# A four-stage transformer kernel: its first batch prepared in two halves at once, the rotation by permuted partitions, and inverse roots in smaller pieces

## The chip, the cores and the metric

The kernel runs on one core of one Trainium2 chip. The metric is device time in microseconds (us), from the first to the last instruction of an execution with what lies around it. Three runs of the kernel before are known, and one more execution was profiled.

## What is computed

The input `x` has 4 batches of 1024 tokens with 128 channels. Six residual blocks follow each other; LN is the layer norm without scale.

```python
x = x + 0.5 * time_mix(LN(x))        # sigmoid(xr @ Wr.T) * (relu(xk @ Wk.T)**2 @ Wv.T); xr, xk mix each token with the one before
x = x + attention(LN(x)) @ proj      # 16 heads of 8, rotary positions, full softmax over 1024 keys
x = x + 0.5 * time_mix(LN(x))
x = x + 0.5 * experts(LN(x))         # rms norm, top 2 of 8 experts, u * silu(gate), plus skip
x = x + linear_attention(LN(x))      # softplus features, running sums
x = x + 0.5 * experts(LN(x))

def apply_rotary(x, cos, sin):
    x1 = x[..., ::2]
    x2 = x[..., 1::2]
    x_rot = jnp.stack((-x2, x1), axis=-1).reshape(x.shape)
    return x * cos + x_rot * sin
```

## The kernel before, in words

**Layout.** `x` stays in SBUF as 32 tiles of 128 tokens. Four tiles are a group of 512 tokens (`g`), two groups a batch. PSUM has 8 banks. Each engine runs its own program in order; a plan made when the kernel is built says which pieces of work come in which order, and every engine walks the same plan and does its share of each piece. Semaphores join the engines. Since each engine is in order, a piece that waits holds everything that stands behind it on its engine.

**The beginning** (`plan_start`, L283 to L298; `pe_start` L987, `dve_start` L1238, `act_start` L1269, `pool_start` L1357, `sp_attention` L1400). First groups 0 and 1 go through the first time mix: statistics, `factors` (VectorE writes variances at L580, GpSimd takes the power -0.5 of them at L593), `mn` (VectorE normalises, L604), `mt` (TensorE turns, L615, ScalarE copies, L747), `mk` (product L686/L687, VectorE clamps at L727, ScalarE squares at L751), `mr` (L692/L693, tanh at L755), `mv` (L698, VectorE L733, GpSimd adds to `x`, L767) and `ms` (statistics). ScalarE then fills four quarters of the score operands with ones (`act_blanks`, L1323 to L1331).

Then the queries and keys of batch 0 are prepared (`attention_queries`, L122). A piece is numbered `i` = 0 to 3: queries of half 0 and 1, keys of half 0 and 1. For each `i` there are two products (`rot`, L779), one for the values and one with swapped weight columns for the rotated neighbour; VectorE adds a bias and multiplies by the cosine or sine (L1131), GpSimd adds the two (`roped`, L1345). Then `split`: the float32 result becomes three bfloat16 parts in rounds. In batch 0 ScalarE rounds (L1289) and VectorE subtracts (L1149); in the other batches VectorE does both (L1154 to L1157). VectorE also squares (L1138), sums the keys (L1140) and takes the longest norm (L1161) from a product (`norms`). In batch 0 the pieces `i` follow one another through one pair of buffers `t_cos`, `t_sin`: a new piece waits until GpSimd has added the one before (L1129). SyncE writes the parts to DRAM (`write_parts`, L1410 to L1413: one transfer for each half-stack of queries, two for keys) and reads them back in the stacked layout of the score products (`stack_parts`, L1421): for batch 0 first two of the eight head pairs of queries and keys, 12 transfers, then the other six pairs, 12 transfers.

`bound` (L1209) works out a bound of the scores, `max` (L962, L1176) a shift for each row; ScalarE sends it to DRAM (L1387) and reads it into the stacked layout (`maxima_in`, L1397; in batch 0 at the piece `max_in`). Behind it stand, in this order, `mn` for groups 2 and 3, the values of batch 0 (`val`), and `mt`, `mk`, `mr`, `mv` for groups 2 and 3.

**Attention** (L997, L1250, L1293, L1364) has 256 steps. A step has two score units on TensorE (L1018, four matmuls), two exponentials of 1024 columns on ScalarE (L1307) and one sum over keys (L1035). Step 8 is the first that needs head pairs 2 to 7. `plan_attention` (L301) puts side pieces into the steps: the queries, keys and values of the next batch, the mixes of other groups, the second time mix, and the routing of the first round of experts. At most two pieces go into a step, and at most one of them may use TensorE. All side products share PSUM bank 7, so that a side product waits until VectorE or ScalarE has read the one before. A `rot` product is cut into two pieces that go into two steps.

**Routing** (`route_part`, L249). `rroot` lets GpSimd take the power -0.5 of two variances for each tile in one instruction (L586, L1675). `rnorm` waits for it, writes two rows of factors for the residual (`keep`, L1538, L1539), and normalises the tiles (L1545); then `rext` turns them on TensorE (L615) and `rscore` scores them (L1489). The linear attention asks for its factors through `lfac` in the same way.

## Time and profile before

| what | value |
|---|---|
| median of three runs | 1231.58 us (1227.18 to 1231.70) |
| the profiled execution, its own time | 1228.77 us |
| its span, from first to last instruction | 1227.0 us |
| mean granted TensorE clock | 0.932 of full speed |
| busy: TensorE, ScalarE, VectorE, GpSimd | 1023.1, 798.9, 602.1, 428.5 us |
| first exponential starts | 84.9 us |
| last exponential starts | 623.2 us |

Busy time counts neither waits nor the issuing of transfers. In the trace's rows PE is TensorE, PEld its weight loads, DVE VectorE, ACT ScalarE, POOL GpSimd, SP SyncE; "ACTq" is the sequencer of ScalarE issuing a transfer. "L1307" is a line of the kernel. A bracket at the end of a row of the timeline gives the time in which the engine stood idle before it, and what released it.

### The profile page before, as it was taken

How to read it: one execution, taken by the hardware profiler on the slowest of the kernel's cores; microseconds unless marked ns; L12 is line 12 of the kernel's file. 1: busy time of each engine (PE TensorE's matmuls, PEld its weight loads, DVE VectorE, ACT ScalarE, POOL GpSimd, SP SyncE). 2: the span in 40 equal slices, each digit the busy share in tenths (PEclk: the TensorE clock that was granted, in tenths of full speed). 3: DMA queues.
4: the chain of work that ended last, by engine and by line, in shares of the span. 5: the costliest groups of instructions: out<-in, count | busy, mean ns of one | idle time of the engine just before them, and what ended most of it. 6: DMA issues, size and time to landing. Idle time of an engine off the chain costs nothing.

```text
span 1227.0 us, 22947 instructions
## 1 busy us (share of the span) xinstructions
PE 1023.1 (83%) x8718; PEld 474.0 (39%) x8718; DVE 602.1 (49%) x1791; ACT 798.9 (65%) x1164; POOL 428.5 (35%) x406
## 2 busy tenths in 40 slices
PE   4479998998999989999978989888889875989930
PEld 3342222322222233222236656644445443665620
DVE  4753565366365234321234525757877943524522
ACT  4439888988899979999953646665455522565510
POOL 4211122221111211454211345544543483455445
PEclk9679999999999999999999989989999987998975
DMA  5180280027127600300101333200000011334422
GB/s 153 39 130 1 52 116 3 2 50 106 15 53 115 187 1 1 126 26 27 31 14 52 98 107 93 80 21 20 17 16 2 14 42 45 108 104 114 121 69 67
DMA packets 84826, 74.74 MB, mean 61 GB/s; under 512 B 11440, under 2 KB 78896, under 8 KB 83824
## 3 DMA queue, kind: packets, MB, share of 16 engines
q1 hardware_dynamic: 74924, 55.48, 19.9%
q0 software_dynamic: 8192, 16.79, 4.7%
q8 instruction: 74, 1.21, 0.4%
q10 hardware_dynamic: 1604, 0.99, 0.3%
q14 instruction: 32, 0.26, 0.1%
HBM read 39.28 MB, written 33.95 MB: 60 GB/s over the span
## 4 chain that ended last, share of the span: by engine, by line
PE 55%; DVE 18%; ACT 12%; POOL 5%; issue 4%; DMA 1%; ACTq 0%; POOLq 0%; SPq 0%; DVEq 0%
PE ps L1035 11%; PE ps L1755 11%; ACT attn_probs L1307 10%; PE ps L1018 6%; PE ps L779 6%; PE ps L1781 5%; PE ps L615 3%; PE ps L1767 2%; POOL moe_back L1700 2%; PE ps L2063 2%; DVE lin_scores L2191 2%; PE ps L1745 2%; PE ps L1987 2%; PE ps L2077 1%; DVE stats L571 1%
## 5 line engine op out<-in xcount | busy, mean ns | idle before, releaser
L1307 ACT ACTIVATE attn_probs<-ps 128x1024 f32<-128x1024 f32 x512 | 484.6, 1063 | 48.1 <-PE ps L1018 46.8
L1035 PE MATMUL ps<-attn_probs,attn_v 128*18 128x512 f32 x2048 | 271.9, 603 | 4.5 <-DVE room L1266 3.9
L1689 POOL DMA_INDIRECT slots<-moe_xr,moe_slot x128 | 125.9, 984 | 141.5 <-ACT attn_probs L1307 51.8
L1018 PE MATMUL ps<-stack 50*128 50x512 bf16 x1024 | 165.5, 387 | 7.4 <-ACT attn_probs L1307 1.3
L1700 POOL DMA_INDIRECT moe_back<-results,moe_slot x128 | 123.6, 965 | 103.8 <-PE ps L1745 43.4
L1755 PE MATMUL ps<-stack,lin_scores 128*128 x312 | 155.4, 621 | 0.0
L1018 PEld LDWEIGHTS ps<-stack 50*128 50x128 bf16 x1024 | 34.3, 94 | 242.9 <-ACT attn_probs L1307 229.1
L1861 ACT ACTIVATE lin_scores<-ps 128x256 f32<-128x256 f32 x156 | 58.4, 382 | 97.8 <-PE ps L1755 97.8
L1834 DVE TENSOR_TENSOR lin_scores<-ps,lin_scores 128x256 f32<-128x256 f32 x156 | 59.0, 419 | 113.7 <-ACT lin_scores L1861 113.6
L1781 PE MATMUL ps<-stack,lin_scores 128*128 x624 | 83.6, 276 | 4.8 <-ACT lin_heads_out L1874 4.8
L1781 PEld LDWEIGHTS ps<-stack,lin_scores 128*128 128x128 f32 x624 | 76.0, 192 | 6.5 <-issue 6.5
L1755 PEld LDWEIGHTS ps<-stack,lin_scores 128*128 128x128 f32 x312 | 56.0, 200 | 40.2 <-issue 40.1
L1035 PEld LDWEIGHTS ps<-attn_probs,attn_v 128*18 128x18 f32 x2048 | 45.7, 97 | 59.8 <-issue 39.0
L1345 POOL TENSOR_TENSOR room<-room 128x512 f32<-128x512 f32 x16 | 22.2, 1389 | 132.8 <-DVE room L1131 132.8
L2261 ACT ACTIVATE lin_scores<-ps 128x512 f32<-128x512 f32 x64 | 34.7, 595 | 42.1 <-PE ps L2063 42.1
L2191 DVE TENSOR_TENSOR lin_scores<-ps,c_causal 128x512 f32<-128x512 f32 x64 | 41.0, 682 | 35.2 <-PE ps L2063 35.2
L1827 DVE TENSOR_SCALAR lin_scores<-ps,c_norm_scale 128x256 f32<-128x256 f32 x80 | 37.9, 474 | 35.0 <-PE ps L1745 34.6
L1767 PEld LDWEIGHTS ps<-c_ident,lin_scores 128*128 128x128 f32 x312 | 38.5, 142 | 37.6 <-issue 35.0
L1131 DVE SCALAR_TENSOR_TENSOR room<-ps,c_attn_b,moe_xr 128x512 f32<-128x512 f32 x32 | 23.9, 749 | 58.9 <-PE ps L779 57.4
L1867 ACT ACTIVATE lin_scores<-ps 128x512 f32<-128x512 f32 x80 | 46.7, 584 | 7.6 <-PE ps L1767 4.8
L571 DVE BATCH_NORM_STATS2 stats<-x 128x6 f32<-128x128 f32 x192 | 41.4, 278 | 20.2 <-POOL x L897 8.8
L1745 PE MATMUL ps<-c_ident,moe_gathered 128*128 128x128 f32 x156 | 33.0, 294 | 20.0 <-DMA moe_gathered<-slots 13.1
(227 smaller groups left out, 1483.0 us busy)
## 6 DMA issues: line engine op xcount, KB each, us to landing
moe_gathered<-slots SPq DMA_DIRECT2D x76, 128.0 KB, 2.4
results<-lin_heads_out SPq DMA_DIRECT2D x76, 128.0 KB, 1.8
stack<-qk_parts SPq DMA_DIRECT2D x36, 256.0 KB, 9.4
qk_parts<-moe_xr SPq DMA_DIRECT2D x32, 128.0 KB, 2.5
qk_parts<-moe_xr SPq DMA_DIRECT2D x16, 192.0 KB, 2.8
stack<-in_expert_w SPq DMA_DIRECT2D x1, 3072.0 KB, 10.6
slots<-zeros SPq DMA_DIRECT2D x1, 3008.0 KB, 11.3
slots<-zeros SPq DMA_DIRECT2D x1, 2496.0 KB, 18.3
```

The costliest lines, as they stand in the source:

```text
L779: instruction = T.matmul(out[cols, :], weights[:, cols], moving, start=True, stop=True)
L1018: instruction = T.matmul(k.ps[:, SCORE_BANKS[i % 3][s], :], d.stack[b % 2][rows, 1, pair, kt * P:(kt + 1) * P], d.stack[b % 2][rows, 0, pa ...
L1035: instruction = T.matmul(k.ps[32 * j:32 * j + STRIP, PV_BANK, :], d.v[:, b % 2, kt, first:first + STRIP], d.probs[:, n % A_PROBS, j * BANK ...
L1307: A.activation(d.probs[:, n % A_PROBS, 2 * e * BANK:2 * (e + 1) * BANK], k.ps[:, banks[0]:banks[1] + 1, :].rearrange("p a n -> p (a n)"), ...
L1689: G.indirect_dma_start(out=k.dram["slots"][half][0:SLOT_TILES[r] * P], out_offset=bass.IndirectOffsetOnAxis(ap=d.slot[:, FIRST[r] + at, c: ...
L1700: G.indirect_dma_start(out=k.back[:, i % RING, c, :], out_offset=None, in_=k.dram["results"][half][0:SLOT_TILES[r] * P], in_offset=bass.In ...
L1755: T.matmul(k.ps[:, bank, :], d.gt[:, u % NB, i, :], w[:, bass.ds(offset[u, i], 2 * HIDDEN)], start=True, stop=True).then_inc(k.full[bank], 1)
L1767: instruction = T.transpose(k.ps[:, bank, at:at + P], d.h[:, u % NB, i, c * P:(c + 1) * P], k.ident[:, :])
L1781: instruction = T.matmul(k.ps[:, bank, i * DIM:(i + 1) * DIM], d.ht[:, u % NB, i, c * P:(c + 1) * P], w[:, 2 * HIDDEN + c * DIM:][:, bass. ...
L1834: V.tensor_tensor(d.h[:, u % NB, i, :], k.ps[:, bank, 0:HIDDEN], d.silu[:, u % NB, i, :], ALU.mult).then_inc(k.free[bank], 1)
L1861: A.activation(d.silu[:, u % NB, i, :], k.ps[:, bank, HIDDEN:2 * HIDDEN], ACT_FN.Silu).then_inc(k.e_silu, 1)
L2191: V.tensor_tensor(d.scores[:, m % NS, :].rearrange("p (j t) -> p j t", j=HPG), k.ps[:, bank, :].rearrange("p (j t) -> p j t", j=HPG), caus ...
```

## The change

All in one edit: (1) `plan_start` orders the beginning by hand. Both halves of a piece go side by side: two normalised buffers, and a second pair of rotation buffers for odd `i` (`rotated`). `split` is replaced in batch 0 by three pieces `cut` for each `i`, all squares and rounds on ScalarE, the subtractions on VectorE; the sum of the keys comes out of a round (`accum_out`). ScalarE copies the turned tiles and normalises groups 2 and 3 (from `shift`, a product made by VectorE), and clamps their `mk`. `mt`, `mk` and `mr` of groups 2 and 3 stand between the rounds, and only `mv` and the values follow `max`. (2) The fills by ScalarE are gone; SyncE writes just two rows of ones for each half of the two stacks, in four transfers. (3) The slots of queries and keys are exchanged, so that keys are written in one transfer for each half-stack. The stacked queries are read as soon as both halves have landed, and the other six pairs are read when the row shifts have landed. (4) In batches 1 to 3 the neighbour comes from `stream_shuffle` on VectorE, not from a second product. (5) Powers are taken in pieces: of at most 4 tiles for the first 8 of a request and then the rest, in routing the needed factor first in pieces of 8 tiles, the factor for `keep` last; the two `keep` rows move from `rnorm` to `rtop`.

```diff
+def first_queries():
+    def rotate(i, which):
+        return [("rot", 0, i, which, 0), ("rot", 0, i, which, 1)]
+    out = [("norm", 0, 0), ("norm", 0, 1), ("shift",), ("xt", 0, 0), ("xt", 0, 1), ("mn", 2), ("mn", 3)]
+    out += rotate(0, 0) + rotate(0, 1) + rotate(1, 0) + rotate(1, 1)
+    out += [("cut", 0, 0), ("cut", 1, 0)] + rotate(2, 0) + [("cut", 0, 1), ("cut", 1, 1)] + rotate(2, 1)
+    out += [("cut", 0, 2), ("cut", 1, 2), ("mt", 2), ("norms", 0, 0)] + rotate(3, 0) + [("mt", 3), ("norms", 0, 1)] + rotate(3, 1)
+    out += [("mk", 2), ("cut", 2, 0), ("mr", 2), ("cut", 2, 1), ("mk", 3), ("cut", 3, 0), ("cut", 2, 2), ("norms", 0, 2)]
+    return out + [("cut", 3, 1), ("norms", 0, 3), ("mr", 3), ("cut", 3, 2)]
...
-    k.start += [piece for _, piece in attention_queries(0)] + [piece for _, piece in attention_maxima(0)]
-    k.start += [("max_in",), ("mn", 2), ("mn", 3)] + [piece for _, piece in attention_values(0)]
-    k.start += [(kind, g) for kinds in (("mt",), ("mk", "mr"), ("mv",)) for g in (2, 3) for kind in kinds]
+    k.start += first_queries() + [("bound", 0), ("max", 0), ("mv", 2), ("mv", 3)] + [piece for _, piece in attention_values(0)]
...
     def rotate(i, which):
-        yield PRODUCT, ("rot", b, i, which, 0)
-        yield SAME_BANK, ("rot", b, i, which, 1)
+        if b and which:
+            yield OTHER, ("rot", b, i, which, 1)
+        else:
+            yield PRODUCT, ("rot", b, i, which, 0)
+            yield SAME_BANK, ("rot", b, i, which, 1)
...
+def root_parts(tiles):
+    cuts = sorted({min(at, tiles.stop) for at in (tiles.start, tiles.start + TPG, tiles.start + 2 * TPG, tiles.stop)})
+    return [slice(*pair) for pair in zip(cuts, cuts[1:])]
...
+            if b and which:
+                dve_need(V, k, k.neighbours_done)
+                V.scalar_tensor_tensor(d.t_sin[:, :], d.t_sin[:, :], bias[:, 2 * qk + 1:2 * qk + 2],
+                                       k.sin[:, half * BANK:(half + 1) * BANK], ALU.add, ALU.mult).then_inc(k.a_turned, 1)
+                return
...
+            if b:
+                k.neighbours_done = dve_mark(k, V.stream_shuffle(d.t_sin[:, :], k.ps[:, bank, :], NEIGHBOUR))
...
+            if part == 0:
+                A.wait_ge(k.a_roped, i + 1)
+                if i >= 2:
+                    bank, n = k.use["norms", 0, i - 2]
+                    A.wait_ge(k.full[bank], n + 1)
+                A.activation(d.square[:, s, :], d.roped[:, s, :], ACT_FN.Square).then_inc(k.a_square, 1)
...
+            if half and not b:
+                parts_landed(b, i)
+                stack_parts(b, qk, slice(0, 2), k.a_stack_first)
         if b == 0:
-            for qk in range(2):
-                parts_landed(b, 2 * qk + 1)
-                stack_parts(b, qk, slice(0, 2), k.a_stack_first)
+            S.wait_ge(k.a_max_in, 32)
             for qk in range(2):
                 stack_parts(b, qk, slice(2, PAIRS), k.a_stack_in[0])
...
-            pool_inverse_root(G, k, d.root[:, :, some], d.root_var[:, :, some])
+            pool_inverse_roots(G, k, [(d.root[:, 1, part], d.root_var[:, 1, part]) for part in parts]
+                               + [(d.root[:, 0, some], d.root_var[:, 0, some])])
```

## Rows read from the trace of the kernel before

**Rows 1.** The page: the costliest group of instructions.

```profile
L1307 ACT ACTIVATE attn_probs<-ps 128x1024 f32<-128x1024 f32 x512 | 484.6, 1063 | 48.1 <-PE ps L1018 46.8
```

**Rows 2.** By stretch: length, busy PE, PEld, DVE, ACT, POOL, granted clock, DMA share, GB/s.

```profile
0.00:84.40 84.40, 41.72 (x191) 31.19 (x192) 45.62 (x137) 30.27 (x29) 20.20 (x22) 0.80 0.48 109
...
139.50:435.00 295.50, 273.81 (x2901) 80.42 (x2901) 151.00 (x412) 263.78 (x282) 58.85 (x43) 0.99 0.39 71
```

**Rows 3.** Timeline of the beginning, until the first rounding: start, duration, instruction, idle before.

```profile
22.26 14.53 ACT L1331 ACTIVATE stack<-pair 32x4096 f32<-32x4096 f32 x4
...
27.40 2.91 POOL L593 TENSOR_TENSOR ln_rstd<-ln_var,minus_half 128x16 f32<-128x16 f32 x1 [1.61 <-DVE ln_var L580]
...
37.33 0.75 DVE L1131 SCALAR_TENSOR_TENSOR room<-ps,c_attn_b,moe_xr 128x512 f32<-128x512 f32 x1 [1.02 <-PE ps L779]
...
39.86 1.26 POOL L1345 TENSOR_TENSOR room<-room 128x512 f32<-128x512 f32 x1 [9.55 <-DVE room L1131]
41.16 0.63 ACT L1289 ACTIVATE moe_xr<-room 128x512 bf16<-128x512 f32 x1 [4.37 <-POOL room L1345]
```

**Rows 4.** The same timeline: last rounding, row shifts, values, last mix, first scores.

```profile
61.45 0.63 ACT L1289 ACTIVATE moe_xr<-room 128x512 bf16<-128x512 f32 x1 [0.76 <-DVE room L1149]
...
66.37 0.48 PE L962 MATMUL ps<-c_ident,attn_neg_max 128*128 128x128 f32 x1 [2.17 <-issue]
...
66.64 3.62 PE L779 MATMUL ps<-c_attn_vo,room 128*128 128x128 f32 x16
...
70.08 1.84 ACTq L1397 DMA_DIRECT2D stack<-row_maxima  x2
...
84.42 1.14 PE L1018 MATMUL ps<-stack 50*128 50x512 bf16 x6 [1.25 <-issue]
```

**Rows 5.** Stretches of 2 us, columns as in rows 2.

```profile
50.00:52.00 2.00, 0.20 (x1) 0.00 (x0) 1.30 (x3) 0.72 (x2) 0.00 (x0) 0.67 0.04 10
...
88.00:90.00 2.00, 2.00 (x10) 0.16 (x8) 1.95 (x13) 2.00 (x3) 0.00 (x0) 0.50 0.53 68
```

**Rows 6.** DMA issues from 40 to 110 us: size of one, median us to landing.

```profile
stack<-qk_parts SPq DMA_DIRECT2D x12, 192.0 KB, 10.5
...
stack<-qk_parts SPq DMA_DIRECT2D x12, 64.0 KB, 2.4
```

**Rows 7.** GpSimd's powers by shape, over the span: count, busy us, mean ns, idle before.

```profile
L593 POOL TENSOR_TENSOR ln_rstd<-ln_var,minus_half 128x8 f32<-128x8 f32 x9 | 14.9, 1655 | 25.6 <-DVE ln_var L580 25.6
...
L593 POOL TENSOR_TENSOR ln_rstd<-ln_var,minus_half 128x4 f32<-128x4 f32 x10 | 10.6, 1057 | 21.2 <-DVE ln_var L580 21.2
```

**Rows 8.** The chain that ended last, in order of time: start, length, what.

```profile
426.51 5.44 POOL moe_root L593
...
660.13 2.92 POOL moe_root L593
...
896.12 1.69 POOL ln_rstd L593
...
1024.43 2.94 POOL moe_root L593
```

**Rows 9.** Timeline of ScalarE: steps 108 to 133, and the first routing.

```profile
324.15 17.66 ACT L1307 ACTIVATE attn_probs<-ps 128x1024 f32<-128x1024 f32 x18 [0.52 <-PE ps L1018]
341.99 31.80 ACT L1307 ACTIVATE attn_probs<-ps 128x1024 f32<-128x1024 f32 x34 [0.17 <-PE ps L1018]
...
434.46 0.60 ACT L1648 ACTIVATE moe_xrt<-ps 128x512 f32<-128x512 f32 x1 [3.08 <-PE ps L615]
```

**Rows 10.** VectorE by line and shape, 140 to 435 us: count, busy us, mean ns.

```profile
L1155 DVE TENSOR_TENSOR room<-room,moe_xr 128x512 f32<-128x512 f32 x22 | 15.9, 725 | 0.8
...
L1157 DVE CAST moe_xr<-room 128x512 bf16<-128x512 f32 x11 | 4.7, 427 | 0.4
...
L1120 DVE COPY room<-ps 128x512 f32<-128x512 f32 x4 | 2.8, 690 | 2.9 <-PE ps L615 2.9
```

**Rows 11.** Timeline of TensorE: one side piece of a rotation product.

```profile
98.96 0.64 PE L779 MATMUL ps<-room,c_qk_w 128*32 128x256 f32 x8
```

More of the change, by code:

```diff
@@ L66 @@
 STACK = 64
+NEIGHBOUR = [(lane // HD ^ 1) * HD + lane % HD for lane in range(32)]
 PAIRS = HEADS // 2
@@ L721, in dve_mix @@
         instruction.then_inc(k.mix_weights, 1)
-    elif kind == "mn":
+    elif kind == "shift":
+        some = slice(DVE_MIXES * TPG, FIRST_MIXES * TPG)
+        V.wait_ge(k.root_out, max(k.root_of[t] for t in range(some.start, some.stop)))
+        V.scalar_tensor_tensor(d.shift[:, :], k.moments[:, some, 0], -1.0, k.rstd[:, some], ALU.mult,
+                               ALU.mult).then_inc(k.mix_shift, 1)
+    elif kind == "mn" and g < DVE_MIXES:
         dve_normalise(V, k, g, d.xn[:, g % 2, :, :], k.mix_xn)
-    elif kind == "mk":
+    elif kind == "mk" and g < DVE_MIXES:
         bank, n = k.use[kind, 0, g]
@@ L742, in act_mix @@
     kind, g = piece[0], piece[1] if len(piece) > 1 else None
-    if kind == "mt":
+    if kind == "mn" and g >= DVE_MIXES:
+        A.wait_ge(k.mix_shift, 1)
+        for i in range(TPG):
+            t = g * TPG + i
+            instruction = A.activation(d.xn[:, g % 2, i, :], k.x[:, t, :], ACT_FN.Identity, scale=k.rstd[:, t:t + 1],
+                                       bias=d.shift[:, t - DVE_MIXES * TPG:t - DVE_MIXES * TPG + 1])
+        instruction.then_inc(k.mix_xn_act, 1)
+    elif kind == "mt":
         b, at = g // 2, (g % 2) * BANK
@@ L911, in side @@
             T.wait_ge(k.a_xn, HALVES * b + piece[2] + 1)
-            pe_turn_group(T, k, piece, lambda i: d.xn[:, i, :])
-        elif kind == "rot":
+            pe_turn_group(T, k, piece, lambda i: d.xn_first[piece[2]][:, i, :] if b == 0 else d.xn[:, i, :])
+        elif kind == "rot" and piece[:4] in k.use:
             _, _, i, which, part = piece
@@ L1115, in side @@
         if kind == "norm":
-            dve_normalise(V, k, HALVES * b + piece[2], d.xn[:, :, :], k.a_xn)
-        elif kind == "xt":
+            dve_normalise(V, k, HALVES * b + piece[2], d.xn_first[piece[2]] if b == 0 else d.xn, k.a_xn)
+        elif kind == "xt" and b:
             half = piece[2]
@@ L1157, in side @@
             V.tensor_copy(d.parts[:, s, place[2], :], d.roped[:, s, :]).then_inc(k.a_parts, 1)
+        elif kind == "cut" and piece[2] < 2:
+            i, part = piece[1:]
+            s, place = i % 2, K_PLACE if i // HALVES else Q_PLACE
+            V.wait_ge(k.a_rounded[s], 2 * (i // 2) + part + 1)
+            V.tensor_tensor(d.roped[:, s, :], d.roped[:, s, :], d.parts[:, s, place[part], :],
+                            ALU.subtract).then_inc(k.a_less[s], 1)
         elif kind == "norms":
```

162 lines of the change are left out of this document (88 added, 74 removed).

## Prediction

> **What bounds the kernel now.** I read the page first, then the busy time by stretch, the timeline up to the first exponential, the chain, and the waits of ScalarE. The costliest group is the exponentials [rows 1]: 512 of them, 484.6 us, all between 84.9 and 624 us, so for 540 of the 1227 us ScalarE's exponentials set the pace, with 48.1 us of idle time between them, nearly all put down to the score products. Two things follow: each us by which the first exponential comes earlier is a us of the kernel, and TensorE's side work counts only where it makes ScalarE wait. Before the first exponential no engine is full [rows 2]: in 84.4 us VectorE is busy 45.6, TensorE 41.7, ScalarE 30.3. That is a chain of short steps. A last kind of place is GpSimd's powers: six of those of 8 columns or more stand in the chain (four are shown, [rows 8]; the others are at 92.4, 1.65 us, and 988.1, 2.95), while everything behind them waits.
>
> **The beginning, part by part.** The first power (8 tiles) is cut into 4 and 4: 1.66 becomes 1.06 [rows 7], so all that follows is 0.6 earlier. The second, of 16 tiles, took 2.91 [rows 3]; now the first 4 tiles are ready after 1.06. It starts at 26.8, ends at 27.9, and VectorE normalises both halves back to back (1.1 us each, to 30.1) since they have two buffers. TensorE turns them by 31.2; ScalarE copies (0.6). At the slow clock a rotation product takes 1.7 us (35.4 to VectorE's start at 37.33 [rows 3], two hops in it), so VectorE has both products of piece 0 at 35.0 and GpSimd adds by 37.1, against 41.1 before: 4.0 earlier. The fills, 14.5 us of ScalarE [rows 3], go; I cost that at nothing, since they ended at 36.8 and ScalarE then sat idle 4.4 us for GpSimd's sum. What they covered is now filled by eight small normalisations, some 3 us, which end at 34.9. Their replacement, four transfers by SyncE, stands behind SyncE's loads (over by 17 us) and before its first parts at 43: 25 us for four transfers, nothing on the path.
>
> From 37.1 ScalarE has 24 instructions up to the last round: four squares, twelve rounds, two copies and two clamps for groups 2 and 3, two squares and two tanh. At 0.64 us (a round takes 0.63 [rows 3]) that is 15.4 us, or 52.5 if it never waited. It will wait: for VectorE's subtraction between rounds (0.73 [rows 10], partly covered by the other half), for GpSimd's sums of pieces 2 and 3, and, being in order, for the `mk` and `mr` products that stand between the rounds. Walking the four queues with these durations I get 58.0 with TensorE at full clock throughout, and 62.4 with it at half clock through `mk` and `mr` of group 2 and `mk` of group 3 (each then 3.4 instead of 1.7 us). The clock fell at 50 to 52 us after TensorE had little to do [rows 5], and the same gap now comes at 41 to 44, before dense work, so I take a point between, 59.5. Before, it was 62.1 [rows 4]: 2.6 us gained, with 8.6 us of mixes already inside.
>
> The way from there to the row shifts is unchanged, 4.3 us (62.1 to 66.4 [rows 4]); the maximum's turn is then at 63.8. Behind it stood 18.0 us: values 3.6, the landing of the shifts, and groups 2 and 3 from `mt` to `mv`, the scores at 84.42 [rows 4]. Now only `mv` twice and the values stand there. At half clock: 0.5 for the turn, 3.7, 3.6, then VectorE 0.9 and 0.5 to start the scores, 9.2 in all. The shifts land at about the same time: 1.1 to VectorE's end, 2.6 for the transfer out, 1.8 to issue two transfers [rows 4], 2.3 to land, 7.8. So scores at 73.0 instead of 84.4: **11.4 us gained**, with ends 8.5 (half clock, 75.9) and 14.3 (full clock, 7.8 behind the maximum, 70.1).
>
> The other six head pairs now wait for the shifts. Before, 12 transfers of 192 KB were issued from 70.7 and the engines were still 53% busy at 88 to 90 us [rows 5], 18 us later; the median landing was 10.5 us, against 2.4 for the small ones [rows 6]. Now the first issue is at about 71.6, the last landing at 89 to 90. Step 8 needs it; before, it came 16.5 us after the first scores, here 89.5. I charge **1 us**, with ends 0 and 3. The keys' own first pairs are no danger: written (1.2), landed (2.5), read (2.9 to issue, 2.4 to land) they are there 9 us after the last round, at 68.5.
>
> **Rotation.** In batches 1 to 3, 24 side pieces of TensorE go, 0.64 us of work each [rows 11]. What one costs ScalarE: in steps 108 to 116, with such a piece in nearly each, two exponentials took 1.96 us, in 117 to 133 1.87 [rows 9], so at least 0.1, 2.4 us in all; at most its own 0.64, 15 us. I take 0.25 each, 6 us: nearer the low row, since other pieces move up into the free steps. VectorE gets 12 shuffles, for which the trace has no row. A copy of the same size out of PSUM takes 0.69 [rows 10]; a lower bound is a cast of this size within SBUF, 0.43 [rows 10], an upper one GpSimd's pass over two operands, 1.26 [rows 3]. I take the copy, the one with the same source, size and engine. At 0.69 VectorE gets 8.3 us more on 151 in 295 [rows 2]: half hidden by idle time, but the side bank is now held for 1.4 instead of 0.75 us, and behind a `split` (six passes) that makes a product late. I charge 1. **Net 5**, ends -3 and 12. The Trainium skill, "VectorE: DVE Perf Modes" (the perf-mode tier table), gives a shuffle one element a cycle, 2400 ns for 2048; by that estimate 0.6 us for 512, and the sum would not move.
>
> **Smaller powers.** At 426.5 us 32 columns took 5.44 [rows 8]; the first part will have 8, 1.66 [rows 7], and the two `keep` instructions (0.25) leave the path: 4.0. ScalarE, which had exponentials in hand, stood idle 3.1 us there [rows 9], and the chain runs through the power, so I count 3.1 at least and take 4.0. At 660, 988 and 1024 us 16 columns become 8: 1.3 each, with `keep` 1.5, 1.7 and 1.5. At 92 and 896 us 8 become 4: 0.6 each. Sum 9.9, all on the chain. GpSimd's total grows (three powers for one), but the rest runs while VectorE normalises. What may be late next is the DMA behind routing, so I take **8.5**, ends 5 and 10.
>
> **The sum.** 11.4 - 1 + 5 + 8.5 = 23.9 us, from the profiled execution's 1228.8 us to **1205 us**. That execution is 2.8 below the median of the three runs, which reach from 1227.2 to 1231.7, so a comparison with the median may look 3 us kinder. A difference over 0.5%, 6 us, can be told here.
>
> **Rivals.**
> A, the half clock. The mixes now come in a gap-filled stretch, TensorE stays at 1.2 GHz, in-order ScalarE waits at `mk` and `mr` and the rounds end at 62.4. For it: the clock fell at 50 to 52 us [rows 5], and its mean up to 84.4 us was 0.80 [rows 2]. Gains 8.5 in the beginning, rotation 2, powers 6, less 1, so 15.5: 1213. The Trainium skill, "TensorE: Matmul & The Clock Gate" (what's actually happening), says that the slow clock is the default and that activity releases it. Chance 0.2.
> B, the late stacks. Twelve large transfers behind the shifts take longer than 18 us or their issue slips; TensorE stands at step 8 for up to 8 us: 1212. Against it: the queue is emptier than before, since the small transfers are over. Chance 0.1.
> C, everything lands. Full clock, 14.3; side work was dearer than I think, 10; powers 10: 1195. Chance 0.15.
> D, slower: a shuffle out of PSUM costs far more than a copy. Its place is steps 6 to 130, its price the queue on VectorE behind bank 7. All else gains 25 (11.4 - 1 + 6 + 8.5), so the kernel is slower from 2.1 us a shuffle if each is fully exposed; at 3 us it would be 36 us against 25, 1240. Against it: the 512-column rows of VectorE stand at 0.43 to 0.73 [rows 10]. Chance 0.04.
> E, it does not do what it says: the freed steps are filled by the plan, the beginning hits a wait that I did not see, and 4 us are left: 1225. Chance 0.06.
>
> **How the numbers follow.** The forecast has 0.45, its own range is 1198 to 1211. With A, B and C the range is 1192 to 1218 and leaves out D, E and the tails of A and B, a little under 2 in 10. Faster by over 0.5%: all but D, half of E and the tails, 0.91; same 0.05; slower 0.04.
>
> **What would show it.** First exponential at 73 to 74 us, the last round at 58 to 60, first GpSimd sum of a rotation at 36. Twelve shuffles near 0.7 us. Idle time before L1307's group down from 48 to about 40 us, no row of 5.4 us among the powers and ScalarE's wait of 3.1 us at the first routing gone. A wait of the scores for a transfer at step 8 would mean B; half clock until 70 us and an idle ScalarE before the tanh of group 2, A. Attention as long as before with more time between products and VectorE would prove the rotation term wrong.

## Result and the profile after

The changed kernel takes **1201.92 us** (median of 4 runs, 1199.60 to 1203.07); the kernel before, on the same chip, 1230.90 (4 runs, 1227.18 to 1231.70). The ratio is 0.9768 with a 95% interval from 0.9753 to 0.9783: 2.3% faster. The profiled execution took 1201.29, its span 1199.5. Forecast were 1205, range 1192 to 1218.

A step is a pair of exponentials. Counted through the timeline of ScalarE, the steps start at (us):

| step | before | after | lead |
|---|---|---|---|
| 0 | 84.9 | 69.7 | 15.2 |
| 8 | 102.8 | 89.9 | 12.9 |
| 40 | 172.6 | 168.5 | 4.1 |
| 80 | 258.4 | 257.0 | 1.4 |
| 128 | 364.5 | 349.6 | 15.0 |
| 158 | 425.8 | 411.2 | 14.6 |
| 168 | 452.6 | 434.5 | 18.1 |
| 255 | 622.3 | 601.0 | 21.4 |
| from the last exponential's start to the end | 603.7 | 597.6 | 6.1 |

So the beginning gained more than forecast, most of it was gone by step 80, it came back by step 128, and routing and the rest added to it.

**The beginning**, timeline after, up to the last rounding, against [rows 3, 4]:

```profile
26.40 3.66 POOL L614 TENSOR_TENSOR ln_rstd<-ln_var,minus_half 128x4 f32<-128x4 f32 x3 [1.61 <-DVE ln_var L596]
...
31.32 3.17 ACT L774 ACTIVATE attn_probs<-x,mix_shift,ln_rstd 128x128 f32<-128x128 f32 x8
34.36 1.27 POOL L1398 TENSOR_TENSOR room<-room 128x512 f32<-128x512 f32 x1 [4.29 <-DVE room L1183]
35.66 0.63 ACT L1341 ACTIVATE room<-room 128x512 bf16<-128x512 f32 x1 [1.16 <-POOL room L1398]
...
55.86 0.62 ACT L1350 ACTIVATE moe_xr<-room 128x512 bf16<-128x512 f32 x1
```

The power of 16 tiles is now cut into 4, 4 and 8 (the row merges the three and names the first one's shape). The first GpSimd sum starts at 34.4 (before 39.9), the last round ends at 56.5 (before 62.1). From there to the scores, TensorE's timeline and ScalarE's queue:

```profile
60.51 0.48 PE L999 MATMUL ps<-c_ident,attn_neg_max 128*128 128x128 f32 x1 [2.20 <-issue]
...
69.23 0.82 PE L1056 MATMUL ps<-stack 50*128 50x512 bf16 x6 [1.30 <-DMA stack<-row_maxima]
...
89.47 0.60 PE L1056 MATMUL ps<-stack 50*128 50x512 bf16 x4 [3.51 <-DMA stack<-qk_parts]
```

The first scores wait last for the row shifts' landing, and start 8.7 us behind the turn of the maxima. The third line is step 8: TensorE stood 3.51 us for the second issue of stacks. The chain has both landings:

```profile
65.35 3.58 DMA stack<-row_maxima
...
73.92 15.51 DMA stack<-qk_parts
```

Twelve issues of 192 KB are 2.36 MB, let go at 68.95, when the shifts are in, and landed at 89.43. By stretch (columns as in [rows 2]; the last two lines are the 4 us behind the wait):

```profile
0.00:69.20 69.20, 40.88 (x190) 31.37 (x191) 36.05 (x120) 22.95 (x43) 21.04 (x24) 0.88 0.41 110
69.20:90.00 20.80, 14.83 (x108) 3.53 (x108) 11.64 (x55) 15.29 (x17) 5.27 (x5) 0.92 0.87 115
...
90.00:92.00 2.00, 2.00 (x26) 0.58 (x24) 0.00 (x0) 1.84 (x2) 0.00 (x0) 0.64 0.04 8
92.00:94.00 2.00, 2.00 (x24) 0.86 (x24) 0.00 (x0) 1.09 (x2) 0.00 (x0) 0.50 0.00 0
```

In the second line the DMA engines are 87% busy at 115 GB/s: 2.36 MB at that rate are 20.5 us, which is 68.95 to 89.4. In the third the granted clock is 0.64 and in the fourth 0.50: behind the wait TensorE ran for a time at the lower of its two levels, 1.2 GHz. ScalarE's timeline shows its own wait at step 8 and the one that follows it:

```profile
82.39 3.90 ACT L1368 ACTIVATE attn_probs<-ps 128x1024 f32<-128x1024 f32 x4 [0.86 <-PE ps L1056]
89.91 1.94 ACT L1368 ACTIVATE attn_probs<-ps 128x1024 f32<-128x1024 f32 x2 [3.61 <-PE ps L1056]
92.91 1.94 ACT L1368 ACTIVATE attn_probs<-ps 128x1024 f32<-128x1024 f32 x2 [1.06 <-PE ps L1056]
```

**The exponentials, the shuffles, the powers**, from the page and the groups by shape:

```profile
L1368 ACT ACTIVATE attn_probs<-ps 128x1024 f32<-128x1024 f32 x512 | 481.3, 1081 | 58.3 <-PE ps L1056 57.9
...
L1181 DVE STREAM_SHUFFLE room<-ps 128x512 f32<-128x512 f32 x12 | 8.9, 741 | 0.0
...
L614 POOL TENSOR_TENSOR ln_rstd<-ln_var,minus_half 128x4 f32<-128x4 f32 x30 | 30.7, 1033 | 61.5 <-DVE ln_var L596 61.5
...
L614 POOL TENSOR_TENSOR moe_root<-moe_root_var,minus_half 128x8 f32<-128x8 f32 x12 | 19.8, 1659 | 10.1 <-DVE moe_root_var L1587 10.0
```

The exponentials' idle time rose, 48.1 to 58.3, but 13.2 of it now is the wait ahead of the first one, 3.9 before; between exponentials it is about the same (45.1 and 44.2). The shuffle took 0.74 us; a power of 4 columns 1.03, of 8 columns 1.66. No power of 32 columns is left, and ScalarE no longer waits 3 us at the first routing.

### The profile page after: what moved, and what is told of

Its sections match the earlier page's. It is cut to its first block, busy times and chain, and to the rows that moved or that the text cites. A ratio compares the mean times of both kernels' runs of the same rounds, so it can differ in the third digit from the quotient of the medians.

```text
span 1199.5 us, 22563 instructions
## 1 busy us (share of the span) xinstructions
PE 1006.0 (84%) x8494; PEld 470.1 (39%) x8526; DVE 602.7 (50%) x1798; ACT 787.4 (66%) x1178; POOL 434.8 (36%) x425
## 4 chain that ended last, share of the span: by engine, by line
PE 52%; ACT 18%; DVE 17%; issue 4%; POOL 4%; DMA 3%; SPq 0%; POOLq 0%; ACTq 0%; DVEq 0%
ACT attn_probs L1368 16%; PE ps L1820 11%; PE ps L1073 9%; PE ps L1846 5%; PE ps L816 5%; PE ps L1056 5%; PE ps L636 3%; PE ps L1832 3%; POOL moe_back L1765 2%; PE ps L2128 2%; DVE lin_scores L2256 2%; PE ps L1810 2%; PE ps L2052 1%; PE ps L2142 1%; DMA stack<-qk_parts 1%
## 5 line engine op out<-in xcount | busy, mean ns | idle before, releaser
L1368 ACT ACTIVATE attn_probs<-ps 128x1024 f32<-128x1024 f32 x512 | 481.3, 1081 | 58.3 <-PE ps L1056 57.9
L1056 PE MATMUL ps<-stack 50*128 50x512 bf16 x1024 | 167.7, 387 | 13.2 <-DMA stack<-qk_parts 3.5
L1073 PEld LDWEIGHTS ps<-attn_probs,attn_v 128*18 128x18 f32 x2048 | 43.2, 97 | 64.8 <-issue 44.8
L614 POOL TENSOR_TENSOR ln_rstd<-ln_var,minus_half 128x4 f32<-128x4 f32 (+1 forms) x31 | 32.4, 1055 | 61.5 <-DVE ln_var L596 61.5
L1810 PE MATMUL ps<-c_ident,moe_gathered 128*128 128x128 f32 x156 | 33.1, 294 | 22.0 <-DMA moe_gathered<-slots 14.6
## 6 DMA issues: line engine op xcount, KB each, us to landing
slots<-zeros SPq DMA_DIRECT2D x1, 3008.0 KB, 12.9
```

The lines of the kernel that those rows point to most:

```text
L1056: instruction = T.matmul(k.ps[:, SCORE_BANKS[i % 3][s], :], d.stack[b % 2][rows, 1, pair, kt * P:(kt + 1) * P], d.stack[b % 2][rows, 0, pa ...
L1073: instruction = T.matmul(k.ps[32 * j:32 * j + STRIP, PV_BANK, :], d.v[:, b % 2, kt, first:first + STRIP], d.probs[:, n % A_PROBS, j * BANK ...
L1368: A.activation(d.probs[:, n % A_PROBS, 2 * e * BANK:2 * (e + 1) * BANK], k.ps[:, banks[0]:banks[1] + 1, :].rearrange("p a n -> p (a n)"), ...
```

## Experiments

The kernels ran in three groups, each on a chip of its own, so each kernel is compared through the kernel before, run beside it: 1242.52 us (17 runs) for e1 to e4, 1229.49 (13 runs) for e0, e5, e8, e9, and 1230.13 (7 runs) for e7, e10, e11, e12. Spans and step times are of one profiled execution each. "Behind it" is the time from the start of the last exponential to the end.

| kernel | median us | ratio [95%] | step 0 | step 158 | last exponential | behind it |
|---|---|---|---|---|---|---|
| after, again (e0) | 1204.25 | 0.9788 [0.9764, 0.9811] | 68.6 | 411.1 | 601.7 | 599.7 |
| e1 products | 1219.51 | 0.9798 [0.9764, 0.9832] | 71.1 | 415.7 | 609.6 | 608.1 |
| e2 routing powers | 1228.87 | 0.9869 [0.9834, 0.9905] | 69.6 | 417.8 | 611.0 | 618.2 |
| e3 no wait | 1222.52 | 0.9821 [0.9788, 0.9853] | 85.4 | 426.8 | 618.7 | 612.0 |
| e4 before, no fills | 1244.45 | 1.0015 [0.9995, 1.0035] | 84.4 | 424.7 | 626.0 | 616.6 |
| e5 mixes behind | 1209.34 | 0.9838 [0.9821, 0.9855] | 77.6 | 416.2 | 606.8 | 600.6 |
| e7 two shuffles | 1213.78 | 0.9856 [0.9826, 0.9885] | 70.8 | 420.7 | 611.4 | 602.5 |
| e8 second part first | **1193.84** | **0.9709** [0.9693, 0.9725] | 70.1 | 405.3 | 595.9 | 596.8 |
| e9 before, wait | 1229.73 | 1.0002 [0.9992, 1.0012] | 84.7 | 425.4 | 622.8 | 603.9 |
| e10 all powers | 1213.54 | 0.9861 [0.9831, 0.9892] | 72.9 | 417.6 | 608.3 | 604.0 |
| e11 ahead | 1199.44 | 0.9758 [0.9741, 0.9774] | 71.0 | 404.7 | 595.3 | 596.7 |
| e12 cut, products | 1200.44 | 0.9767 [0.9744, 0.9789] | 69.2 | 407.0 | 599.6 | 598.4 |

Two limits of this table. The profiled execution of e3, 1232.53 us, was the slowest of its five; the other four took 1218.61 to 1223.34. And the changed kernel has no run in the third group. e11, which differs from e8 only in the order of its transfers and has the same span within 0.7 us, has a ratio 0.0049 higher (6 us). So a comparison across groups, as of e7 and e10 with e0 or of e12 with e8, may be off by as much, and is held against the step times below.

**e0, the changed kernel again.** No edit.

> The changed kernel again, beside the kernels of this call, since chips differ by some us. Every theory: 0.977 of the kernel before, first exponential at 69.7 us of the trace, step 8 at 89.9 after a wait of 3.6 us.

Measured: 0.9788, step 0 at 68.6, a wait of 3.38 us at step 8 (88.5). The first exponential moves by 1.1 us from one execution to another.

### What makes the start early

**e4** is the kernel before with its fills done by four DMAs.

```diff
-        if piece == ("mr", 1):
-            act_blanks(A, k)
...
+            S.dma_start(stack[row:row + MAX_ROWS, 1, :, :].rearrange("p r (n c) -> p (r n) c", c=P), ones).then_inc(k.a_blank, 16)
```

> The kernel before with one thing changed: ScalarE's four fills replaced by SyncE's four transfers of ones. My theory: nothing, within 0.1% of the kernel before, since ScalarE only waits behind the fills. Rival: the fills slow VectorE or GpSimd by the memory they share, and the beginning is 1 to 3 us shorter without them.

Measured: no difference that the runs can tell, first exponential at 84.4. 14.5 us of ScalarE's work at the start were free, as the prediction had them.

**e3** takes the wait for the row shifts out of SyncE's queue, so that the second issue of stacks goes ahead of them. SyncE's own rows are written all the same; the scores wait for all they read.

```diff
-            S.wait_ge(k.a_max_in, 32)
```

> The changed kernel without SyncE's wait for the row shifts ahead of the stacks of pairs 2 to 7. In the changed kernel ScalarE stands idle 3.6, 1.1 and 0.6 us at steps 8 to 10, and the chain runs through that transfer. My theory: the twelve large transfers are issued from 62.7 us, land by 82, ahead of step 8, and the kernel is 4 to 5 us faster than the changed one, about 1197.5. Rival: they then stand in the way of the shifts (two small transfers), so that the first scores come later by what step 8 gains: 1201 to 1203.

Measured: the first exponential at 85.4, 15.7 later than in the changed kernel, although the turn of the maxima comes only 0.3 later. Its chain:

```profile
62.02 2.73 DMA row_maxima<-c_same_head
...
66.01 18.54 DMA stack<-row_maxima
84.55 0.14 issue
84.69 0.62 PE ps L1056 x2
```

The second of two transfers of 32 KB, issued at 66.01, took 18.5 us, against 3.6 with the wait. Seven of the twelve large stack transfers had been issued on SyncE's queue by then, the other five followed up to 68.8, and the shifts landed at 84.55, the last stack at 85.08. So it is not only the bytes ahead of them: the shifts were in almost last. Step 8 does not wait here, and in this execution the start lost stays lost: the last exponential is at 618.7, 16.9 later. But the ratios of all runs put e3 only 0.003 to 0.005 above the two measurements of the changed kernel, 4 to 7 us, with overlapping intervals, and this execution was 10 us above the median of its own five. Whether the shifts land as late in the other four is not known.

**e9** asks the opposite: is the wait alone enough? It is the kernel before with that one line added in front of its second issue of stacks.

```diff
+            S.wait_ge(k.a_max_in, 32)
             for qk in range(2):
                 stack_parts(b, qk, slice(2, PAIRS), k.a_stack_in[0])
```

> The kernel before with the one wait added: SyncE's queue issues the second part of the stacks only once the shifts have landed. Theory 'two locks': TensorE works through the mixes until 83.2 anyway, so the first exponential stays at 84 to 85 and the time within 0.4% of the kernel before; with e3 (mixes ahead, no wait: 85.4) this says that neither part alone brings anything. Rival 'the shifts' landing alone held the start': first exponential 2 us or more earlier, at the end of TensorE's mixes plus nothing (82 to 83), 2 us faster. Rival 'late stacks': the second part lands after step 8 (102.8) and the kernel is slower by 1 to 4 us; issued from about 76 and landing some 20 later (96), it should not.

Measured: 1.0002, first exponential at 84.7. TensorE still has its mixes up to 83, in front of the scores in its queue:

```profile
81.67 1.16 PE L698 MATMUL ps<-c_mix_w,attn_probs 128*128 128x128 f32 x8 [0.78 <-DVE attn_probs L733]
84.11 1.32 PE L1018 MATMUL ps<-stack 50*128 50x512 bf16 x6 [1.28 <-issue]
```

**e5** puts the mixes of groups 2 and 3 back behind the turn of the maxima in the changed kernel; the wait stays.

```diff
-    out += [("cut", 0, 2), ("cut", 1, 2), ("mt", 2), ("norms", 0, 0)] + rotate(3, 0) + [("mt", 3), ("norms", 0, 1)] + rotate(3, 1)
+    out += [("cut", 0, 2), ("cut", 1, 2), ("norms", 0, 0)] + rotate(3, 0) + [("norms", 0, 1)] + rotate(3, 1)
...
-    k.start += first_queries() + [("bound", 0), ("max", 0), ("mv", 2), ("mv", 3)] + [piece for _, piece in attention_values(0)]
+    k.start += first_queries() + [("bound", 0), ("max", 0)] + [piece for _, piece in attention_values(0)]
+    k.start += [(kind, g) for kinds in (("mt",), ("mk", "mr"), ("mv",)) for g in (2, 3) for kind in kinds]
...
```

> The changed kernel with the mixes of groups 2 and 3 (transposes, ranks, values) behind the turn of the maxima, where the kernel before had them; the wait of SyncE's queue for the shifts stays. Theory 'two locks': the start needs both, the mixes out of the way and the shifts ahead of the large transfers. Then the shifts land at about 65 but TensorE works through some 17 us of mixes (66.4 to 83.7 in the kernel before) from about 60.5 on: first exponential at 77 to 80, step 8 without a wait because the stacks landed meanwhile, and 5 to 8 us above the changed kernel. Rival 'the wait alone did it' : first exponential at 69 to 72 here too, time within 2 us of the changed kernel. Rival 'mixes only moved': ScalarE has the mixes' work to do either way and what is gained at the start is lost to idle time later, so the end differs by under 2 us although the start is 8 later.

The edit has one more part, not shown above: ScalarE reads the shifts in (`maxima_in`) right behind sending them out, ahead of the mixes, so that they land at 65.3. Measured: first exponential at 77.6, 9.0 later than e0. The stacks are in before step 8, so the wait of 3.4 us there is gone. Of the 9.0, 2.4 come back up to step 8 and 1.5 more up to step 80; the last exponential is 5.1 later, the time 5.1. With e3, e9 and this one the start is a lock with two keys. Mixes ahead, shifts ahead: 69.7. Mixes ahead alone: 85.4. Shifts ahead alone, in the old order: 84.7. In these executions each key alone moved the start by nothing. The other 7 us of the lead, 77.6 against 84.7, are what else the beginning has: both halves side by side, the smaller power, fewer waits between rounds; of these only the power was taken back by itself (e10 below, 3.1 to 4.3 us).

### The wait at step 8

**e8** cuts the second issue of stacks in two. Pairs 2 and 3 land on a semaphore of their own, which TensorE asks for at step 8; pairs 4 to 7 follow, asked for at step 16.

```diff
+            T.wait_ge(k.a_stack_second, STACK_IN)
+        if b == half == kt == 0 and group == 2:
             T.wait_ge(k.a_stack_in[0], STACK_IN)
...
             for qk in range(2):
-                stack_parts(b, qk, slice(2, PAIRS), k.a_stack_in[0])
+                stack_parts(b, qk, slice(2, 4), k.a_stack_second)
+            for qk in range(2):
+                stack_parts(b, qk, slice(4, PAIRS), k.a_stack_in[0])
...
```

> The changed kernel with the second issue of stacks cut in two: pairs 2 and 3 (12 transfers of 64 KB) right behind the shifts, pairs 4 to 7 (12 of 128 KB) behind them, and TensorE waits for the first part at step 8 and for the second at step 16. Theory 'the last landing holds step 8': the 3.6 us wait at step 8 goes, its 1.1 us follower at step 9 with it; step 8 at 86 to 87, step 16 about 4 earlier, and 1 to 4 us of it left at the end (side work crowds steps 19 to 40, so part of the lead may be given back there). Rival 'side work sets the pace to step 40': step 8 is 3.6 earlier but step 40 is not, and the time is within 1 us of the changed kernel. Rival 'the second part now lands after step 16': the wait only moves there; 12 large transfers issued by about 79 and landing 10 to 15 later would be in by 94, before step 16 at 103, so this one is unlikely.

Measured: 1193.84 us, **10.4 less than e0** beside it, far more than any theory had. Of the spans' 8.7, 5.8 stand up to the last exponential and 2.9 behind it. ScalarE's timeline:

```profile
82.99 5.87 ACT L1370 ACTIVATE attn_probs<-ps 128x1024 f32<-128x1024 f32 x6 [0.53 <-PE ps L1058]
89.06 11.78 ACT L1370 ACTIVATE attn_probs<-ps 128x1024 f32<-128x1024 f32 x12 [0.21 <-PE ps L1058]
101.25 7.44 ACT L1370 ACTIVATE attn_probs<-ps 128x1024 f32<-128x1024 f32 x8 [0.41 <-PE ps L1058]
```

Neither step 8 nor step 16 waits. Step 0 to step 8 takes 16.8 us instead of 19.9, step 8 to 40 74.3 instead of 78.6; from there on the two keep their distance. (e8's first exponential was 1.5 later than e0's, so its lead is 5.9 at step 40 and 5.8 at 158 and not 7.4.) So the uncut transfer cost 3.1 up to step 8, about the wait itself, and 4.3 more behind it: the waits at steps 9, 20 and 36, 1.0 to 1.2 each in e0, are gone with it, and the granted clock from 90 to 115 us is 1.00 against 0.91. How the 4.3 divide between the clock and those waits is not shown.

**e11** is e8 with pairs 2 and 3 issued ahead of the wait, and only pairs 4 to 7 behind it (the edit is against e8).

```diff
+            for qk in range(2):
+                stack_parts(b, qk, slice(2, 4), k.a_stack_second)
             S.wait_ge(k.a_max_in, 32)
-            for qk in range(2):
-                stack_parts(b, qk, slice(2, 4), k.a_stack_second)
```

> The kernel with the second issue of stacks cut in two (pairs 2 and 3, pairs 4 to 7), but pairs 2 and 3 (12 transfers of 64 KB) issued ahead of the wait for the shifts, only pairs 4 to 7 behind it. Theory 'bytes in the rings hold the shifts': without any wait 2.3 MB (12 of 192 KB) stood ahead of them and they landed 18.5 us after their issue; here 0.77 MB are issued by about 65 and are nearly through when the shifts are issued, so the shifts land 4 to 8 us after their issue, the first exponential is at 70 to 74, and the time is within 2 us of the kernel that has both behind the wait or up to 4 above it. Rival 'any transfer of stacks in flight holds them as long': first exponential at 80 to 85 and 8 or more above.

Measured: the shifts land 4.62 us after their issue, the first exponential is at 71.0. So 0.79 MB in twelve transfers around them held them by 1 us, 2.36 MB in twelve by 15; in both cases about half of the twelve had been issued before the second shift transfer (six here, seven in e3). The time is unclear: the profiled span is 1192.0, as in e8, but that was the fastest of five runs, the median is 1199.44 (1193.88 to 1201.18), and the ratio lies above that of e8 beyond both intervals, on another chip. I don't claim either order of the two.

### Rotation

**e1** is the changed kernel with the second product back in all batches; **e12** does the same to e8, where no wait at step 8 is in the way.

```diff
-        if b and which:
-            yield OTHER, ("rot", b, i, which, 1)
-        else:
-            yield PRODUCT, ("rot", b, i, which, 0)
-            yield SAME_BANK, ("rot", b, i, which, 1)
+        yield PRODUCT, ("rot", b, i, which, 0)
+        yield SAME_BANK, ("rot", b, i, which, 1)
...
-                k.neighbours_done = dve_mark(k, V.stream_shuffle(d.t_sin[:, :], k.ps[:, bank, :], NEIGHBOUR))
...
```

> The changed kernel with the rotation of batches 1 to 3 by a second product again, in the plan and on the engines. My theory: the 24 side pieces of TensorE cost ScalarE some 6 us and the shuffles gave 1 back, so this kernel is 5 us slower than the changed one, about 1207, with the first exponential still at 69.7 us. Rival: the rotation gave nothing, because the shorter plan crowds the side work and VectorE is late instead (ScalarE waits 2 to 3 us at steps 19, 31, 34 and 35 in the changed kernel): 1201 to 1203.

> The kernel with the second issue of stacks cut in two, and the rotation by a second product in all batches, as the kernel before had it. Without the wait at step 8 the rotation's worth is read by itself. Theory of the prediction's term: 3 to 7 us above the kernel with the stacks cut and the shuffles (ratio to the kernel before 0.974 to 0.977). Rival 'the shuffle's 0.74 eats it': the same within 2 us. Rival 'it was more': over 8 above, since 24 pieces of TensorE's side work also pushed others into stalls.

Measured: e1 lies 0.001 to 0.003 of the ratio above the two measurements of the changed kernel, inside the intervals. e12 against e8 is clearer: 6.6 us by the medians, 7.1 by the ratios (0.0058 of 1230), 5.3 by the spans, 3.7 up to the last exponential, 4.6 from step 0 to 255. The medians and ratios cross groups; against e11, on its own chip, e12's median is only 1.0 higher. The step times are the firmer figure. Four kernels side by side, each with one part more than the one to its left (us of the step times):

| from step to step | before | e12: + start, powers | e8: + shuffles | e0: + stacks uncut |
|---|---|---|---|---|
| up to 0 | 84.9 | 69.2 | 70.1 | 68.6 |
| 0 to 80 | 173.5 | 170.6 | 181.0 | 188.2 |
| 80 to 158 | 167.4 | 167.2 | 154.2 | 154.2 |
| 158 to 255 | 196.6 | 191.7 | 189.8 | 189.8 |
| from the start of step 255 to the end | 604.6 | 599.3 | 597.7 | 600.6 |

This is where the lead went by step 80 and where it came back. The shuffles make the first 80 steps 10.4 us slower and the next 78 13.0 faster: the plan has fewer products to place and sets the others earlier (the last rounding of batch 3's keys falls into step 124 instead of 131). So the total moves little and its place much. The uncut stacks cost another 7.3. e12 has the exponentials at the old rhythm:

```profile
L1360 ACT ACTIVATE attn_probs<-ps 128x1024 f32<-128x1024 f32 x512 | 484.6, 1064 | 52.9 <-PE ps L1055 51.5
```

Its 484.6 us are those of [rows 1], to the tenth.

**e7** does each shuffle twice, the second over the first.

```diff
+                dve_then(V, k, V.stream_shuffle(d.t_sin[:, :], k.ps[:, bank, :], NEIGHBOUR))
                 k.neighbours_done = dve_mark(k, V.stream_shuffle(d.t_sin[:, :], k.ps[:, bank, :], NEIGHBOUR))
```

> The changed kernel with each of its 12 shuffles done twice, one behind the other: 12 times 0.74 us of VectorE more, 8.9 in all, and the PSUM bank that the shuffle reads is held 0.74 longer. Theory 'VectorE has room in attention': under 3 us above the changed kernel (ratio to the kernel before up to 0.981), the extra time lying in idle time of VectorE. Rival 'VectorE's chain holds TensorE in the crowded steps 19 to 40': step 0 to step 158, 341.5 us in the changed kernel, becomes 346 to 350, and the time is 5 to 9 above.

```profile
L1181 DVE STREAM_SHUFFLE room<-ps 128x512 f32<-128x512 f32 x12 | 8.9, 740 | 0.0
...
L1182 DVE STREAM_SHUFFLE room<-ps 128x512 f32<-128x512 f32 x12 | 8.7, 729 | 0.0
```

Measured: 0.9856, which is 8.4 us above e0 by the ratio; step 0 to step 158 takes 349.9 us, against 342.5 in e0 and 341.5 in the changed kernel. By the step times, 7.4 to 8.4 of the 8.7 us of added shuffles came out, most of it (5.8 against e0) in the first 80 steps. The rival's size is right, though VectorE is busy only half of the time (161.0 of 295 us in the changed kernel from 115 to 410). Its mechanism, that VectorE's chain holds TensorE's bank and with it the scores, fits; the run lengthens both VectorE's work and the bank's hold, and does not tell them apart.

### Powers

**e2** joins routing's powers again (both halves in one instruction); **e10** also the norms'.

```diff
-            pool_inverse_roots(G, k, [(d.root[:, 1, part], d.root_var[:, 1, part]) for part in parts]
-                               + [(d.root[:, 0, some], d.root_var[:, 0, some])])
+            pool_inverse_roots(G, k, [(d.root[:, :, some], d.root_var[:, :, some])])
...
-    cuts = sorted({min(at, tiles.stop) for at in (tiles.start, tiles.start + TPG, tiles.start + 2 * TPG, tiles.stop)})
-    return [slice(*pair) for pair in zip(cuts, cuts[1:])]
+    return [tiles]
...
```

> The changed kernel with the powers of the routing in one instruction of both roots again (the keep factors stay where the change put them). My theory: 3.8 us at the first routing and 1.3 at each of three later ones come back, 7.7 in all: about 1209.5. Rival: what the powers gave was swallowed by the transfers behind the routing, and only the first counts: 1205 to 1206.

> The changed kernel with every power whole again, those of the norms (16, 12 and 8 columns in one instruction) and those of routing (both halves joined), as in the kernel before. Theory of the prediction's term: 5 to 10 us above the changed kernel. Rival from the earlier run with routing's powers alone joined, in which step 158 came 6.6 us later than in the changed kernel and step 255 9.3 later: 10 to 14 us above (ratio 0.985 to 0.989), 8 to 9 of it around the first routing (steps 152 to 168) and 2 to 5 behind attention. Rival 'norms alone are the term': step 255 as in the run with the joined routing powers (610.5 there), and only the part behind attention longer.

Measured: e10's ratio is 0.9861, 9.0 us above e0 (0.0073 of 1230) and 11.4 above the first measurement of the changed kernel (0.0093). Its beginning is 3.1 to 4.3 later (72.9; the power of 16 columns is back, 2.91 us); steps 0 to 152 are 2.4 shorter than in e0 (327.1 against 329.5). Then 4.7 is lost between steps 152 and 158 (17.7 us against 13.0), at this chain, which the changed kernel does not have:

```profile
404.91 0.09 DVE moe_root_var L1589
405.00 0.07 issue
405.07 5.44 POOL moe_root L616
410.51 0.03 issue
410.54 1.12 DVE moe_xr L1602 x4
```

From there to step 255 e10 and e0 take the same (189.8). Behind the last exponential it is 604.0 against 597.6 and 599.7. In the first group e2 lost more at the first routing, 6.9 from step 152 to 158 and 1.3 more up to 168. The clock is part of it: in e2 it stood at 0.50 in each stretch of 4 us from 408 to 420.

```profile
412.00:416.00 4.00, 4.00 (x20) 2.07 (x20) 0.19 (x1) 1.94 (x2) 0.00 (x0) 0.50 0.00 0
416.00:420.00 4.00, 4.00 (x23) 1.00 (x16) 0.00 (x0) 2.21 (x3) 0.00 (x0) 0.50 0.00 0
```

That is e2; and this is e10, whose clock was at 1.00 again by the second stretch:

```profile
412.00:416.00 4.00, 4.00 (x23) 1.46 (x21) 0.67 (x3) 1.45 (x2) 0.00 (x0) 0.64 0.00 0
416.00:420.00 4.00, 3.94 (x31) 1.13 (x30) 0.19 (x1) 3.43 (x6) 0.00 (x0) 1.00 0.00 0
```

Why e2's stayed down is not shown.

## Why the prediction was right, term by term

| term | predicted | measured | by |
|---|---|---|---|
| beginning | -11.4 (-8.5 to -14.3) | -15.2 | first exponential |
| step 8 | +1 (0 to 3) | +7.3 from step 0 to 255, +10.4 between medians | e8 against e0 |
| rotation | -5 (+3 to -12) | -4.6 from step 0 to 255, -6.6 between medians | e12 against e8 |
| powers, behind the beginning | -8.5 (-5 to -10) | -4.7 at routing, -4.3 to -6.4 behind attention | e10 |
| first 80 steps, same pieces | none | -2.9 | e12 against before |
| fills | 0 | 0 | e4 |
| sum | -23.9 | -29.0 (medians), -27.5 (spans) | |

**The beginning** was 3.8 better than forecast, 0.9 beyond the better end of its term. The working said: first sum ready at 37.1, last round ended at 59.5, scores at 73.0. It was 35.6, 56.5 and 69.2. The first 1.5 are VectorE's: GpSimd's sum could start at 34.4. The walk through the four queues at full clock allowed 20.9 us for the rounds (37.1 to 58.0), and 20.8 is what they took (35.66 to 56.48); the 1.5 added for the half clock was not due. The clock did fall at 42 to 46, as the forecast had it for 41 to 44, but it was up at 0.95 in the next 2 us and at 1.00 from 48 on, while the first dense products ran (`mk` of group 2, 45.1 to 47.5, took 2.4 us where 1.7 or 3.4 were reckoned with):

```profile
44.00:46.00 2.00, 2.00 (x6) 1.22 (x5) 0.98 (x2) 0.00 (x0) 0.00 (x0) 0.50 0.85 200
46.00:48.00 2.00, 2.00 (x10) 1.28 (x9) 0.13 (x1) 0.42 (x1) 1.26 (x1) 0.95 0.77 183
48.00:50.00 2.00, 2.00 (x14) 1.55 (x14) 0.00 (x0) 1.97 (x6) 0.00 (x0) 1.00 0.19 55
...
64.00:66.00 2.00, 2.00 (x12) 2.00 (x11) 0.41 (x1) 0.00 (x0) 0.77 (x1) 0.50 0.04 4
```

So **rival A** fell. The Trainium skill, "TensorE: Matmul & The Clock Gate" (what's actually happening), has the clock released by activity; the trace agrees, 0.50 at 44 to 46 us with TensorE busy throughout, then 0.95, and 1.00 from 48 to 58. The walk was worth more than the allowance on top of it. From 60 to 66 us, behind little work on TensorE (0.4 us in 56 to 60), the clock was at 0.50 again, as the forecast's last stretch had it. 4.0 and 8.7 to the turn and to the scores (4.3 and 9.2 forecast) gave the rest.

What the prediction did not see is why the start could move at all. It counted the landing of the shifts as 7.8 behind the maximum, "about the same time" as the rest, with 2.3 for the landing itself. No row gave it that: in the kernel before the second shift transfer took 7.5 us, to 78.8, 12.4 behind the turn, and only the mixes up to 83 hid it. The prediction did not say that without the wait in SyncE's queue the shifts could hold the scores until 84.6 (e3). It treated that wait only as a cost, the 1 us at step 8. That the number held without this reasoning is in part luck: the change had both keys.

**Step 8** is the term that failed. The landing was forecast at 89 to 90 and was 89.43, but by two errors that cancel: the transfers were issued at 68.95 and not at 71.6, and took 20.5 us and not 18. The 18 came from DMA engines still 53% busy at 88 to 90 us [rows 5]; in the same trace the first of the twelve is issued at 70.4 and the last lands at 92.4, 22 us. And the need was put 16.5 us behind scores at 73.0, so at 89.5, and scores came at 69.2; the need was at 86, the landing did not move with it, and 3.5 us of the better start were given back on the spot. About as much again was lost behind it: half clock at 90 us, then waits at steps 9, 20 and 36. The term was mis-sized in three ways: the transfers' time was read too short, the need depended on the start's own error, and a wait of TensorE was priced at its length. **Rival B** had its mechanism right (the twelve large transfers took longer than 18 us, and the scores waited at step 8). It allowed a wait of up to 8 us; the wait was 3.5 and its whole cost 7.3. It did not show as 1212 because the start and the powers gave more.

**Rotation**: the net was right and both of its parts were too low. The shuffle took 0.74 where the copy's 0.69 was taken. The estimate of 0.6 that the prediction worked out from the Trainium skill, "VectorE: DVE Perf Modes" (the perf-mode tier table), was under both. But the charge of 1 us for twelve, "half hidden by idle time", is refuted: 8.7 us more of them cost some 8 (e7). If the first shuffle of a pair costs what the second does, the 24 side pieces were worth some 12 to 15 us, near their upper end of 15 (0.64 each) and not 6. That last number is argued from e7 and e12, not measured alone; a second shuffle stands directly behind the first, and the first might have had more cover. The prediction's sign, idle time between exponentials down from 48 to about 40 us, did not come: without the wait ahead of the first it was 44.2 and is 45.1. **Rival D** asked for 2.1 us a shuffle and had 0.74. Its condition, that each is fully exposed, came nearly true for the added ones.

**Powers**: 9.0 to 11.1 where 8.5 were forecast and 9.9 was the sum of the rows. The first routing was to give 4.0; it gave 4.7 in steps 152 to 158 (e10). The four behind attention were to give 5.3 before the discount; with all powers whole that part is 4.3 to 6.4 longer. That part differs by as much between kernels with the same powers (see Open), so whether the discount for "the DMA behind routing" was needed is not settled.

**The sum** came out 3.1 under the forecast, inside its own range of 1198 to 1211. The start was 3.8 better and step 8 6.3 dearer than forecast. The terms as measured by steps add up to 24.4 to 26.5 of the 27.5 us between the spans; 2.9 of them are a term that the prediction lacked. **Rival C** had the start and the powers about right, but the wait at step 8 took back what it needed for 1195. e12 has the products' old pieces and yet runs the first 80 steps in 170.6 us instead of 173.5. The mixes of groups 2 and 3 are over before the first scores in both, so it is not their work. 1.3 of the 2.9 lie in the first 8 steps (16.6 us against 17.9), where the granted clock was 0.90 in e12 and 0.81 before, with a stretch at 0.50 in both (the one before is in [rows 5]). That this is the cause is argued, not tested, and the other 1.6 is open.

**Open.** The stretch behind the last exponential differs by up to 5.8 us (596.7 to 602.5, the first group left out) in kernels of one kind of powers, with the same work in it; so 2.9 of e8's 10.4, 6.1 of the change's own lead and the powers' share behind attention carry this uncertainty. Why the plan with shuffles is slower in steps 0 to 80 by 10.4, beyond VectorE's share, was not taken apart. A version with e8's cut and a plan that keeps side work out of the first 80 steps was not tried.

## What to carry to other kernels

- Before a start is moved, list everything it waits for, one landing time each, and ask for each transfer what other bytes are in flight when it is issued. What ends last hides the others: in the kernel before, the mixes up to 83 hid a landing at 78.8, and with the mixes alone moved the scores waited for a landing at 84.6 (e3). Only the change that moved both showed anything.
- When a large transfer is held back for a small urgent one, cut it by the time of need: the first third here was needed at step 8, the rest 16 us later, and the cut gave 9 to 10 us (e8 against e0 on one chip, 1193.84 against 1204.25).
- A wait of TensorE can cost more than its length: 3.1 to 3.5 us here cost 7.3, with half clock and further waits behind it; and an engine that is half idle over a stretch can still be almost fully exposed (e7).

## What the runs showed of the hardware

- The second of two transfers of 32 KB on ScalarE's queue landed 3.1 to 3.8 us after its issue with nothing large in flight (3.6 in the changed kernel), 4.6 when six of twelve transfers of 64 KB had just been issued on SyncE's queue (e11), 7.5 and 10.7 when two of twelve of 192 KB had (the kernel before, e4), and 18.5 when seven of those twelve had (e3). A queue of one's own did not get them past. In e11 and the kernel before the same 0.39 MB stood ahead, so the bytes ahead alone do not set the time; in e3 and e11 the shifts landed 0.5 and 0.9 us before the last of the twelve. (Issue and landing times are those of the issues and of the semaphores' updates in the traces.)
- 2.36 MB in twelve transfers took 20.5 us from first issue to last landing in the changed kernel, 115 GB/s at 87% busy DMA engines, and 22.0 in the kernel before and in e3.
- A shuffle of 128x512 from PSUM took 0.74 us, one of 128x512 already read once just before, 0.73.
- Reading ScalarE's accumulator behind a rounding took 0.19 us; it is an instruction of its own in the timeline:

```profile
53.45 0.19 ACT L1348 ACTIVATION_READ_ACCUMULATOR moe_xr<-room 128x1 f32 x1
```
